# A new written order for the opening of a causal attention kernel, zeros stored in 39 pieces, and later transposes of q and k

## What is computed

```
q, k, v = (x @ w_qkv) in 16 heads of 32
q, k = unit_norm(q), unit_norm(k)
q, k = rope(q), rope(k) on every second head
logits = q @ k.T * q_gain, causal
x = layernorm(x + softmax(logits) @ v @ w_out)
# 8 experts, 2 for each token, and a shared one
x = layernorm(x + experts(x))
```

## Time and profile before

| | |
|---|---|
| median of 3 runs | 1262.27 us (1262.16 to 1262.39) |
| profiled execution, its own time | 1263.19 us |
| its span | 1261.4 us |
| PE busy | 1127.5 us, 89% |
| PEld busy | 798.4 us, 63% |
| DVE busy | 610.3 us, 48% |
| ACT busy | 544.4 us, 43% |
| POOL busy | 499.9 us, 40% |
| opening, to the first scores | 74 us |
| attention | up to 660 us |

### The profile page before, as it was taken

The page is one execution under the profiler, slowest core; times in us unless marked ns, Lnnn a source line. Parts: engine busy times, 40 slices in busy tenths (PEclk is TensorE's granted clock), DMA queues, the critical chain, the costliest instruction groups (busy, mean ns, idle before and its releaser), DMA issues.

```text
span 1261.4 us, 19831 instructions
## 1 busy us (share of the span) xinstructions
PE 1127.5 (89%) x6618; PEld 798.4 (63%) x6619; DVE 610.3 (48%) x1120; ACT 544.4 (43%) x894; POOL 499.9 (40%) x360
## 2 busy tenths in 40 slices
PE   5459899998979989998989999598999999999984
PEld 5446355654545545564337887367899999997763
DVE  2424876368553675645845846122222222222774
ACT  3226775566655666656852541011222332321131
POOL 1002555046340463422863206725246464622530
PEclk9869999999999999999988999789999999999997
DMA  5952502334131341324406302833244453412341
GB/s 144 367 148 70 139 11 84 101 84 117 51 101 44 84 125 43 101 59 125 144 1 207 117 1 85 310 105 92 95 143 153 135 166 127 146 59 76 107 160 67
DMA packets 90621, 141.73 MB, mean 112 GB/s; under 512 B 12272, under 2 KB 36848, under 8 KB 90544
## 3 DMA queue, kind: packets, MB, share of 16 engines
q1 hardware_dynamic: 74320, 103.48, 27.1%
q10 hardware_dynamic: 10944, 19.93, 4.6%
q0 software_dynamic: 5280, 17.31, 4.2%
HBM read 84.59 MB, written 56.10 MB: 112 GB/s over the span
## 4 chain that ended last, share of the span: by engine, by line
PE 64%; DVE 16%; issue 8%; POOL 4%; ACT 3%; DMA 2%; SPq 1%; another core or an unknown queue 1%; ACTq 0%; DVEq 0%; POOLq 0%
PE scores L497 12%; PE bank L1134 9%; PE scores L1166 7%; PE bank L490 7%; PE scores L554 5%; PE bank L1191 5%; PE bank L585 5%; PE scores L414 3%; PE bank L1188 3%; POOL key_sum L1493 3%; ACT probs L1292 2%; PE scores L512 1%; DVE key_sum L1407 1%; DVE x L861 1%; DMA turn_scratch<-turned_l 1%
## 5 line engine op out<-in xcount | busy, mean ns | idle before, releaser
L1292 ACT ACTIVATE probs<-scores,shift_now 128x1024 f32<-128x1024 f32 (+3 forms) x320 | 299.3, 985 | 132.8 <-PE scores L1166 62.5
L1166 PE MATMUL scores<-q_stack,k_stack 96*128 96x512 f32 (+3 forms) x640 | 205.7, 425 | 22.3 <-DMA k_stack<-turn_scratch 13.8
L1166 PEld LDWEIGHTS scores<-q_stack,k_stack 96*128 96x128 f32 x640 | 116.0, 198 | 155.3 <-issue 74.8
L1493 POOL TENSOR_TENSOR key_sum<-key_sum,probs 128x512 f32<-128x512 f32 (+2 forms) x76 | 154.4, 2031 | 128.1 <-ACT probs L1292 124.4
L1407 DVE TENSOR_TENSOR key_sum<-key_sum,probs 128x1536 f32<-128x1536 f32 (+2 forms) x76 | 157.0, 2066 | 42.7 <-ACT probs L1292 40.8
L1191 PE MATMUL bank<-probs,v_sb 128*32 128x512 f32 (+3 forms) x1280 | 152.4, 548 | 0.0
L497 PE MATMUL scores<-ffn_w,xt_h 128*128 x624 | 131.9, 334 | 4.6 <-issue 4.5
L964 POOL TENSOR_TENSOR ffn_w<-raw,ones 128x1408 fp32r<-128x1408 f32 (+2 forms) x36 | 71.6, 2000 | 150.7 <-PE bank L490 103.3
L554 PE MATMUL scores<-x1T_h,ffn_w 128*128 128x512 f32 (+1 forms) x384 | 104.2, 403 | 11.3 <-issue 8.9
L497 PEld LDWEIGHTS scores<-ffn_w,xt_h 128*128 128x128 f32 x624 | 103.4, 190 | 13.7 <-issue 11.7
L554 PEld LDWEIGHTS scores<-x1T_h,ffn_w 128*128 128x128 f32 (+1 forms) x384 | 69.1, 182 | 37.2 <-issue 13.5
(11 more groups left out here) (207 smaller groups left out, 1835.5 us busy)
## 6 DMA issues: line engine op xcount, KB each, us to landing
q_stack<-turn_scratch SPq DMA_DIRECT2D x48, 256.0 KB, 3.9
k_stack<-turn_scratch SPq DMA_DIRECT2D x48, 256.0 KB, 3.9
x_sorted<-zeros SPq DMA_DIRECT2D x1, 9984.0 KB, 28.9
y_sorted<-y_tile ACTq DMA_DIRECT2D x39, 256.0 KB, 2.2
x_tile<-x_sorted ACTq DMA_DIRECT2D x37, 256.0 KB, 2.7
turn_scratch<-turned_h SPq DMA_DIRECT2D x32, 256.0 KB, 2.9
turn_scratch<-turned_l SPq DMA_DIRECT2D x32, 256.0 KB, 3.1
raw<-w_gate SPq DMA_DIRECT2D x8, 704.0 KB
```

Source lines behind the costliest of these rows:

```text
L1166: mm = nc.tensor.matmul(scores[:, p, hh, lo:CH], k_stack[0:3 * HD, h, j * P:(j + 1) * P], q_stack[0:3 * HD, i % 2, h, lo:CH], start=True, ...
L1292: nc.scalar.activation(probs[:, slot % 4, 2 * p:2 * p + 2, lo:CH], scores[:, p, :, lo:CH], ACT.Exp, bias=shift_now[:, p:p + 1]).then_inc(e ...
L1493: nc.gpsimd.tensor_tensor(key_sum[:, 3, lo:CH], key_sum[:, 3, lo:CH], new, ALU.add).then_inc(sum_pool, 1)
```

## The change

Loads: x has a buffer for each of its 16 tiles (12 in `x_early`, four in `x_late`). SyncE issues x tile 0, the weights, the 15 other tiles, and then the tables as two DMAs. GpSimd's split of the weights no longer waits for the tables.

Opening: one list, `OPENING`, gives TensorE and ScalarE the order of x tiles, projections (p) and turns (t). The first projection stands behind x tile 0. Tiles 12 to 15 of x are transposed in slots 4, 5 and 6 of group 0 (`LATE_X_AT`), through the bank `turn_ps`. The squares of chunk 1 have a buffer of their own in group 0.

Zeros: 39 DMAs of 256 KB, one in each of 13 slots of the groups 0, 1 and 2. Their source is 128 columns wide, so they move in rows of 512 B.

Turns: q and k of a chunk are turned in slots apart. Those of chunk 1 of the next group go over to slots 0 and 2 of that group (2 and 3 in group 0). `DIRECT` loses slots 14, 15, 28 and 29 and gains 13 and 22.

```diff
 PROJECT_AT = {(2, 0): 1, (2, 1): 2, (2, 2): 3, (2, 3): 4,
-              (1, 0): 32, (1, 1): 32, (1, 2): 34, (1, 3): 35}
+              (1, 0): 31, (1, 1): 32, (1, 2): 33, (1, 3): 34}
...
-                (1, 0): 36, (1, 1): 37}
-TURN_AT = {(2, 0): 8, (2, 1): 9,
-           (3, 0): 15, (3, 1): 16,
-           (0, 0): 31, (0, 1): 32,
-           (1, 0): 38, (1, 1): 39}
+                (1, 0): 35, (1, 1): 36}
+TURN_AT = {(1, 0): 0, (1, 1): 2,
+           (2, 0): 9, (2, 1): 13,
+           (3, 0): 18, (3, 1): 22,
+           (0, 0): 33, (0, 1): 36}
...
-DIRECT = set(range(STEP_AT[1])) | {4, 5, 6, 10, 11, 14, 15, 23, 28, 29, 30, 36, 38, 39}
+DIRECT = set(range(STEP_AT[1])) | {4, 5, 6, 10, 11, 13, 22, 23, 30, 36, 38, 39}
...
+FIRST_TURN_AT = (2, 3)
+EARLY = 3 * TPC
+LATE_X_AT = {4: [12], 5: [13, 14], 6: [15]}
+OPENING = [("x", 0), ("p", 0), ("x", 1), ("x", 2), ("p", 1), ("x", 3), ("x", 4), ("p", 2), ("x", 5), ("x", 6),
+           ("p", 3), ("x", 7), ("x", 8), ("p", 4), ("x", 9), ("p", 5), ("x", 10), ("p", 6), ("t", 0), ("t", 1),
+           ("x", 11), ("p", 7)]
+FILL_AT = [4, 5, 6, 7, 11, 14, 15, 16, 25, 26, 27, 28, 29]
...
-            sp.wait_ge(zero_made, 1)
-            sp.dma_start(xs_dram.rearrange("(j p) d -> p j d", p=P), zeros[:].unsqueeze(1).broadcast_to([P, MAX_TILES, D])).then_inc(zero_filled, 16)
...
+                    if g < NG - 1 and slot in FILL_AT:
+                        sp.wait_ge(scores_ready, 2 * (SLOTS * g + slot))
+                        fill_zeros(len(FILL_AT) * g + FILL_AT.index(slot))
                     if slot == LOAD_W_AT:
-                        sp.wait_ge(turned, 2 * (4 * g + 4))
+                        sp.wait_ge(turned, 2 * (NC * g + 3))
+                        sp.wait_ge(q_roped, 2 * (NC * g + 4))
+                        sp.wait_ge(k_roped, 2 * (NC * g + 4))
...
-            if tt == 0 and (later(g) or c):
+            if tt == 0 and (later(g) or c >= 2):
                 nc.scalar.wait_ge(q_roped, 2 * C)
                 nc.scalar.wait_ge(k_roped, 2 * C)
...
-            if not later(g) and slot == 3:
-                nc.scalar.wait_ge(zero_filled, 16)
             if not later(g) and slot == 0:
-                nc.scalar.wait_ge(x_turned, NT)
+                nc.scalar.wait_ge(x_turned, EARLY)
...
-            pool.wait_ge(tables_loaded, 16 * (2 * NC + 1))
             pool_split_w(0)
+            pool.wait_ge(tables_loaded, 48)
```

More of the change, by code:

```diff
@@ L88, in work_at @@
 def work_at(table, slot, g):
-    if table is TURN_AT and isinstance(g, int) and g == 0 and slot == 0:
-        for which in range(2):
-            yield 0, 1, which
+    if table is TURN_AT and isinstance(g, int) and g == 0 and slot < TPC:
+        if slot in FIRST_TURN_AT:
+            yield 0, 1, FIRST_TURN_AT.index(slot)
+        return
     for (c, part), at in table.items():
@@ L1136, in pe_project, with pe_turn_x @@
             mm.then_inc(qkv_done, 1)
+        def pe_turn_x(t):
+            nc.tensor.wait_ge(x_loaded[t], 16)
+            if t == EARLY:
+                nc.tensor.wait_ge(turn_low, 4)
+            elif t > EARLY:
+                nc.tensor.wait_ge(xT_low, t)
+            elif t >= 4:
+                nc.tensor.wait_ge(xT_low, t - 3)
+            for k in range(KC):
+                mm = nc.tensor.transpose(xT_bank(t)[:, k * P:(k + 1) * P], x_tile_in(t)[:, k * P:(k + 1) * P], ident[:])
+            mm.then_inc(x_turned, 1)
         def pe_turn(g, c, which):
             C = NC * g + c
+            if not later(g) and c == 2:
+                nc.tensor.wait_ge(xT_low, NT)
             if which == 0:
@@ L1233, in group @@
                         pe_turn(*work)
+                    if not later(g):
+                        for t in LATE_X_AT.get(slot, []):
+                            pe_turn_x(t)
                     if slot or later(g):
@@ L1239, in _, with squares_of, act_x_high @@
             tail_tensor(pe)
+        def squares_of(g, c):
+            return squares_second if not later(g) and c == 1 else squares
+        def act_x_high(t):
+            nc.scalar.wait_ge(x_turned, t + 1)
+            nc.scalar.copy(xT_h[:, :, t * P:(t + 1) * P], xT_bank(t).rearrange("p (k n) -> p k n", k=KC)).then_inc(xT_high, 1)
         def act_copy_qkv(g, c, tt):
@@ L1322, in group @@
                         act_turn_high(*work)
+                    if not later(g):
+                        for t in LATE_X_AT.get(slot, []):
+                            act_x_high(t)
             each_group(act, group)
@@ L1450, in _ @@
-            for which in range(2):
-                dve_turn_low(0, 0, which)
+            for t in range(8):
+                dve_x_low(t)
+                if t == 0:
+                    dve_split_w(0)
+            dve.wait_ge(tables_loaded, 16 * (3))
+            nc.vector.tensor_scalar(gain_abs[:], gain[:], -1.0, None, ALU.mult).then_inc(shift_steps, 1)
+            dve.wait_ge(shift_steps, 1)
+            nc.vector.tensor_tensor(gain_abs[:], gain_abs[:], gain[:], ALU.max).then_inc(shift_steps, 1)
@@ L1452, in _ @@
+            dve_norms(0, 0)
+            for t in range(8, EARLY):
+                dve_x_low(t)
+                if EARLY - 3 <= t < EARLY - 1:
+                    dve_turn_low(0, 0, t - EARLY + 3)
             dve_norms(0, 1)
@@ L1486, in pool_add_keys @@
                 nc.gpsimd.wait_ge(sum_pool, added(g, slot) - 1)
+            if not later(g) and slot == first_added(ADDING[0]):
+                nc.gpsimd.wait_ge(x_turned, NT)
             if slot == first_added(i) and (later(g) or i > ADDING[0]):
```

125 lines of the change are left out of this document (58 added, 67 removed).

## The result

The changed kernel takes 1.0040 of the time of the kernel before, 95% interval 1.0020 to 1.0059: a median of 1267.69 us (1265.08 to 1269.29, 5 runs) against 1262.27 (1259.94 to 1264.84, 5 runs). It is slower by 5.4 us, where 4.7 us less were forecast. The time lies in the range given (1243 to 1268), but the sign is wrong. The profiled execution took 1265.08 us, its span 1263.0; it was the fastest of the five.

What follows compares the result with a forecast made beforehand. Opening bound by transfers and a chain, TensorE waiting in groups for turns and GpSimd's additions; terms -23.0 + 0.7 + 7.5 - 12.5 + 1.0 + 21.6 = -4.7 us, giving 1257.6 us from the median 1262.3, range 1243 to 1268.

Steps and rivals of the forecast that it cites:

- opening: Before the first scores of group 0: earlier weights, norm and q turn bring scores at 51.1; -23.0 us, bounds -19 and -25.
- slots 0 to 4 of group 0: Turns move from slot 0 to slots 2 and 3, q of chunk 1 is stacked late; +0.7 us, bounds -2 and +3.
- x in slots 4 to 6 (to slot 9): Group 0: four late x transposes, idling at their one bank and a lower clock; +7.5 us, bounds +4 and +9.
- q of chunk 2 at slot 12: q turned in slot 9, needed in slot 12, with a chain about as long; +1 us, bounds 0 and +4.
- slots 8 to 24: Idle turns go, a gap comes in slot 14; -2.3 us in group 0, -3.4 in others, -12.5 in all.
- handover: Slot 28 to slot 4 of the next group, three times: waits in slot 32 and for k_stack; +21.6 us, bounds +8 and +30.
- end of group 3: Slots 28 and 29 change, but GpSimd's split of w_out holds slot 31 as before; 0, bounds -2 and +3.
- Rivals (2): Between groups: handover costs nothing new because k_stack is ready sooner or the norm begins earlier; 1239, or 1243 to 1247; chance 0.18.
- (4): Slots 12, 18 and the weights' load, three groups: zero pieces hold up the stacks; up to 8 us, 1266; chance 0.14.
- rival (3): Behind the gaps in slots 14 and 32 and at handovers: TensorE's lower clock costs more; 1273, half of it 1265; chance 0.18.
- signs of being wrong: Slot 0 of group 1 under 14 us after the norm of chunk 1 begins, or the opening gaining less than 19.
- Hidden: Zero pieces in groups 0 to 2 cost 0; slots 28 and 29 in group 3 cost 0, bounds -2 and +3.

Runs made afterwards that it cites:

- k_turn_35: Changed kernel with the k turn of the next group's chunk 0 moved from slot 36 to slot 35; 0.9887 of the kernel before.
- direct_28_29: Changed kernel with slots 28 and 29 put back into DIRECT; 0.9884 of the kernel before.
- old_handover: Changed kernel with slots 28 and 29 back in DIRECT and projections, norms and turns at the groups' end as before; 0.9874 of the kernel before.
- after_again: The changed kernel timed and profiled once more, nothing changed; 1.0045 of the kernel before.
- sums_at_14: Changed kernel with slot 14 in DIRECT in place of slot 13; 1.0061 of the kernel before.
- x_in_opening: The kernel best with x tiles 12 to 15 transposed in the opening instead of slots 4 to 7; 0.9655 of the kernel before.
- best: Changed kernel with k turn at slot 35, slots 28, 29 and 37 added to DIRECT, one x tile per slot; 0.9697 of the kernel before.
- zeros_in_group_3: Changed kernel with all 39 zero pieces in 13 slots of group 3, three per slot; 1.0048 of the kernel before.
- busy_wait_38: Changed kernel with 38 extra matmuls on TensorE ahead of the first scores of groups 1, 2 and 3; 1.0061 of the kernel before.

## Why the prediction was wrong

The stages of the changed kernel's first profile against the terms (from the exponentials above, and ScalarE's v copy of slot 25 where a stage ends there):

| term | forecast | measured |
|---|---|---|
| opening | -23.0 | -21.4 |
| slots 0 to 4 of group 0 | +0.7 | +1.4 |
| x in slots 4 to 6 (to slot 9) | +7.5 | +8.8 |
| q of chunk 2 at slot 12 | +1.0 | +1.7 |
| slots 8 to 24 | -12.5 | -10.3 |
| handover | +21.6 (9.0, 3.6, 9.0) | +20.5 (9.7, 1.9, 8.9) |
| end of group 3 | 0 | +3.3 |
| sum (of unrounded terms) | -4.7 | +3.8 at slot 39 |

**The waits and their causes were right, but for one.** k_turn_35 and direct_28_29 show the two causes of the handover's loss: the written order puts the norm ahead of the k turn (19.6 us), and two additions delay the norm and with it GpSimd's rotation, the squares and slot 32 (most of the 20 us). The new handover without these two waits is worth 18.8 us, which is why the changed kernel loses only about half of their 39.8. From old_handover to the changed kernel the loss is 21.6 us timed; that this is the very number of the forecast is chance, since the end of group 3 is part of it. Rivals (2) and (4) fall. Of rival (3), the half clock behind the waits is there, 0.79 and 0.68 in the windows, but a wait for `k_stack` cost 2.1 us in clock where that could be measured. The forecast had charged 3.7 for it, and the rival 2.5 more. The Trainium skill (TensorE: Matmul & The Clock Gate, Loop structure matters more than you think) says that a wait of 8 us for a DMA takes the clock to half; the trace agrees: behind the wait of 8.29 the first score matmul took 0.79 us, at full clock 0.50, and the mean over 10.3 us was 0.79 of the full clock. Neither of the signs of being wrong that the prediction named appeared: slot 0 of group 1 came 16.0 us after the norm, and the opening gained 21.4.

**That the handover's total came out was in part luck.** Counted from ScalarE's v copy of slot 25, the norm of chunk 1 began 4.5, 3.4 and 4.2 us later than before in groups 0, 1 and 2, where the forecast had 1.9 each time. The 16.0 us from the norm to the first scores came as forecast. Against that, from the first scores to the exponential of slot 4 it took 2.8 us more, 2.1 less and 2.8 more, where 4.8, 1.4 and 4.8 more were forecast: the clock stood at 0.79 behind the wait, not near 0.5. The two errors cancel.

**The sum failed in its sizes, and one cost stood at nothing.** It is a difference of -35.5 and +30.8. The gains came out 3.8 us smaller and the costs 4.7 larger, and this miss of 8.5 us in all turned its sign. The steps that failed are the 0 for the end of group 3 (3.3 us), the size of "Slots 8 to 24" (2.2) and that of the opening (1.6); the x tiles and the two small terms cost 2.7 more, and the handover 1.1 less.

The largest single miss is in "Hidden": "In group 3 slots 28 and 29 also change, but there GpSimd's long split of w_out holds slot 31 as before: 0, bounds -2 and +3". The split does hold slot 31, whose exponential waits for the addition of slot 27 behind it. But the split itself got longer: VectorE now adds slots 28 and 29 while it runs. The changed kernel first, then the kernel before:

```profile
619.54 18.33 DVE L1451 TENSOR_TENSOR key_sum<-key_sum,probs 128x1536 f32<-128x1536 f32 x5
...
630.20 6.06 POOL L985 TENSOR_TENSOR wo_l<-wo_raw,wo_h 128x2048 fp32r<-128x2048 f32 x1
...
639.37 2.12 ACT L1331 ACTIVATE probs<-scores,shift_now 128x1024 f32<-128x1024 f32 x2 [8.96 <-POOL key_sum L1539]
```

```profile
618.98 10.48 DVE L1407 TENSOR_TENSOR key_sum<-key_sum,probs 128x1536 f32<-128x1536 f32 x3
...
629.64 4.56 POOL L978 TENSOR_TENSOR wo_l<-wo_raw,wo_h 128x2048 fp32r<-128x2048 f32 x1
...
635.80 2.12 ACT L1292 ACTIVATE probs<-scores,shift_now 128x1024 f32<-128x1024 f32 x2 [5.07 <-POOL key_sum L1493]
```

In all eight profiles without 28 and 29 in DIRECT the low part of w_out takes 6.05 or 6.06 us and the small split behind it 1.76; in all eight with them, where VectorE is idle meanwhile, they take 4.56 or 4.57 and 0.25 or 0.26. direct_28_29 changes nothing but this set, and there slot 31's exponential comes 22.1 us after slot 24's, not 25.1. From group 3's `pe_sums` of step 2 to slot 39 the changed kernel is 3.3 us behind the kernel before (4.5 in after_again). For slots 24 to 37 of group 3 the eight profiles without 28 and 29 have 41.3 to 43.1 us, the seven with the new opening that have them 37.6 to 39.3.

The next is "Slots 8 to 24". Group 0 was forecast -2.3 and measured -2.5; groups 1 and 2 were forecast -3.4 each and measured -1.5 and -2.5. The 1.1 that I added there for the clock (0.79 over 8 us) was not regained: over the 10 us around the wait of 3.03 us in slot 14 the clock is at 0.68, so the loss had moved to another slot. Without that wait (sums_at_14) slots 12 to 24 are 1.8 and 2.7 us shorter, but nothing is gained in all, since VectorE's norm and outputs, and behind them the split of the weights, come no sooner.

Group 3 measured -3.8 up to its `pe_sums`, where -3.4 was forecast.

In the opening the first projection ended at 13.3, not at 12, and the norm came at 29.0, not 26.8. The last two projections of chunk 0 followed at 3.3 us each (3.4 were forecast), but the second took until 19.6: it waited for the split of x tile 1 and began at half clock (1.62 us for four matmuls instead of 0.96). The late x tiles cost 1.3 more than forecast, and x_in_opening, against best, shows that 5 to 6 us of their cost were due to their place alone.

**What stays open.** The first profile is 3.8 us behind at the end of attention and 1.6 at the end of the span, the medians 5.4; the second was 9.6 behind at the end of attention. Single profiles don't settle the last 2 to 4 us, and the two timed values for step 2 (11.2 and 4.5) agree only within their intervals.

## What to carry to other kernels

When a chain feeds the next stage (here turn, cast, subtract, store, read back), look in each engine's written order for long work ahead of its links: one slot of difference was 20 us. An addition given to an engine "with room" costs its length wherever something is queued behind it, here a norm, a rotation, squares and a bank. It can also lengthen the work of another engine beside it, here GpSimd's split by 3.0 us. Where a forecast is a small difference of large gains and costs, its sign is not known better than their bounds. Build the parts apart: the new opening alone gave 0.991, and the whole, with the waits behind it taken out, gave 0.9655.

## What the runs showed of the hardware

A zero piece of 256 KB lands in 3.3 us, in the page's DMA issues of the changed kernel, and moving the pieces to group 3 made no difference (1.0048 against 1.0045):

```profile
x_sorted<-zeros SPq DMA_DIRECT2D x39, 256.0 KB, 3.3
```

The Trainium skill (DMA: Bandwidth & Descriptors, Measured) asks for 1 MiB or more in a DMA. No run here compares 39 pieces with the one DMA in the same kernel; what zeros_in_group_3 shows is that no wait depends on where they stand.

The same operation of GpSimd, 128x2048 with two inputs, took 4.56 us while VectorE was idle and 6.06 while VectorE added beside it (the split of w_out above).

I had not expected that 7 us of fillers, ended 3 us before the scores, leave the clock as low as idling all the time does: 0.79 us for a score matmul of slot 0 in both (busy_wait_38 and the changed kernel, group 1).

The kernel before was 1.4 and 1.6% faster in two groups of runs than in the others. In the profiles taken with those two the stages of attention are like the others', and the part from the last exponential on took 583 to 590 us instead of 602 to 608. The groups ran on different chips; the cause stays open.
